# Four result buffers for the second layer, and a bias table loaded from two queues

## The reference, cut to what matters

```python
def _L0_conv_ref(x, qkv_w, qkv_b, proj_w, proj_b, rel_table):   # shifted-window attention
    bias = rel_table[idx].reshape(L, L, HEADS).transpose(2, 0, 1)      # L = 49, HEADS = 12
    xs = jnp.roll(x, shift=(-SHIFT, -SHIFT), axis=(1, 2))
    ...                                                     # windows of 7 x 7 tokens, 96 channels
    attn = jnp.einsum('bhqd,bhkd->bhqk', q * d ** -0.5, k) + bias[None] + mask
    out = jnp.einsum('bhqk,bhkd->bhqd', softmax(attn), v) @ proj_w.T + proj_b
    ...                                                     # rolled back
def _L1_conv_ref(x):
    s = box_sum(x, 2, 5)                                    # 5 places along the width
    num = box_sum(s * s, 3, 20)                             # 20 channels
    d = box_sum(box_sum(x * x, 2, 5), 3, 20)
    return jnp.nan_to_num(num / (d * norm), nan=1.0)

x = x + _L0_conv_ref(_gn(x), ...)          # x: (32, 56, 56, 96) float32, group norm per image
x = x + _L1_conv_ref(_gn(x))
```

## Time and profile before

| | |
|---|---|
| time, median of 3 runs | 3396.27 us (3393.39 to 3396.65) |
| the profiled execution: its time | 3382.73 us |
| its span, first to last instruction | 3380.9 us |
| PE busy | 3166.0 us, 94% of the span |
| DVE, ACT, POOL busy | 2784.9, 2375.2, 2263.3 us |
| mean granted TensorE clock | 0.982 |
| transfers in `q1` (all issued by SP) | 270.81 MB, 32.8% of 16 engines |

### The profile page before, as it was taken

One profiled execution on the slowest core, in us unless ns is written; L12 is line 12 of the kernel. 1 busy time (PEld: TensorE's weight loads), 2 busy tenths in 40 slices (PEclk: granted clock), 3 DMA queues, 4 the chain that ended last, 5 costly groups with the idle time before them and its releaser, 6 DMA issues.

```text
span 3380.9 us, 146870 instructions
## 1 busy us (share of the span) xinstructions
PE 3166.0 (94%) x60544; PEld 2620.4 (78%) x60544; DVE 2784.9 (82%) x4882; ACT 2375.2 (70%) x4705; POOL 2263.3 (67%) x2522
## 2 busy tenths in 40 slices
PE   3999999999999999999999999999999999999997
PEld 2778787887888778787778787778777777787785
DVE  4788888888888888888888888888888888888883
ACT  2567776777777777777777777777777777777764
POOL 3566666666677666677666667666667666677663
PEclk8999999999999999999999999999999999999995
DMA  3333333333333333333333333333333333332220
GB/s 74 82 89 80 87 92 77 85 89 84 87 91 84 84 93 80 84 93 81 84 93 80 87 92 81 83 93 81 85 92 81 84 92 81 86 92 71 73 63 23
DMA packets 385693, 280.20 MB, mean 83 GB/s; under 512 B 261927, under 2 KB 384904, under 8 KB 385032
## 3 DMA queue, kind: packets, MB, share of 16 engines
q1 hardware_dynamic: 385032, 270.81, 32.8%
HBM read 39.35 MB, written 38.54 MB: 23 GB/s over the span
## 4 chain that ended last, share of the span: by engine, by line
PE 47%; SPq 26%; DVE 8%; issue 6%; ACT 6%; DMA 5%; POOL 1%; DVEq 0%; ACTq 0%; POOLq 0%
SPq L317 10%; SPq L325 10%; PE pP L466 9%; PE pO L481 8%; PE pS L454 6%; DMA out<-tok_out 5%; SPq L330 5%; PE pM L555 3%; DVE T L816 3%; PE pM L549 3%; PE pM L566 3%; PE pM L504 3%; PE pM L394 2%; PE pM L388 2%; PE pM L436 2%
## 5 line engine op out<-in xcount | busy, mean ns | idle before, releaser
L1052 POOL TENSOR_TENSOR T<-T,MX 128x588 f32<-128x588 f32 x1024 | 1213.0, 1185 | 602.8 <-DVE MX L823 599.5
L816 DVE TENSOR_TENSOR T<-pS,table 128x588 f32<-128x588 f32 x1024 | 781.6, 763 | 353.8 <-PE pS L454 352.4
L663 ACT ACTIVATE P<-pP 128x588 f32<-128x588 f32 x1024 | 674.8, 659 | 258.7 <-PE pP L466 231.0
L466 PE MATMUL pP<-K,T 113*128 113x113 f32 x6144 | 789.4, 264 | 14.6 <-POOL T L1052 8.4
L823 DVE TENSOR_REDUCE MX<-T 128x12 f32<-128x588 f32 x1024 | 775.0, 757 | 17.9
L481 PE MATMUL pO<-V,P 128*49 128x18 f32 x24576 | 697.7, 198 | 46.1 <-ACT g L696 39.9
L481 PEld LDWEIGHTS pO<-V,P 128*49 128x49 f32 x24576 | 662.8, 126 | 53.0 <-ACT g L696 45.1
L466 PEld LDWEIGHTS pP<-K,T 113*128 113x128 f32 x6144 | 630.3, 143 | 71.0 <-issue 23.2
L1017 POOL TENSOR_TENSOR y<-Y 96x472 f32<-96x472 f32 x224 | 217.1, 969 | 491.6 <-ACT Y L740 491.6
L454 PE MATMUL pS<-KE,QS 128*64 128x196 bf16 (+1 forms) x8192 | 474.9, 233 | 19.8 <-DMA KE<-KS 13.5
L454 PEld LDWEIGHTS pS<-KE,QS 128*64 128x64 bf16 x8192 | 302.0, 109 | 135.4 <-issue 81.6
(11 more groups left out here) (94 smaller groups left out, 5904.0 us busy)
## 6 DMA issues: line engine op xcount, KB each, us to landing
KE<-KS SPq DMA_DIRECT2D x512, 147.0 KB
KS<-knh SPq DMA_DIRECT2D x768, 49.0 KB, 2.0
QS<-qnh SPq DMA_DIRECT2D x768, 49.0 KB
out<-tok_out SPq DMA_DIRECT2D x384, 84.0 KB
tok_in<-x SPq DMA_DIRECT2D x224, 84.0 KB
KS<-knl SPq DMA_DIRECT2D x384, 49.0 KB, 2.0
QS<-qnl SPq DMA_DIRECT2D x384, 49.0 KB
tok_in<-x SPq DMA_DIRECT2D x224, 63.0 KB
```

Source lines behind the costliest of these rows:

```text
L466: mm = pe.transpose(pP[:, c, QN * at:QN * at + QN], T[j % 4][0:QN, 2 * h:2 * h + 2, :], pick)
L663: act.activation(P32[j % 3][:, :, :].rearrange("p (c a w) q -> p c a (w q)", c=2, w=2), src, ACT.Exp).then_inc(p_made, 1)
L816: dve.tensor_tensor(T[j % 4][:, :, 0:L].rearrange("p (b h) k -> p b h k", b=2), pS[:, :, 0:HALF].rearrange("p b (h k) -> p b h k", k=L), t ...
L1052: pool.tensor_tensor(t, t, MX[j % 4][:, :].unsqueeze(2).broadcast_to([128, HEADS, L]), ALU.subtract).then_inc(shifted, 1)
```

## The change

There are four `tok_out` buffers and four `stored` semaphores instead of two; `result(G)` now waits for the stores of group G-4. SP issues four of the small transfers that start the semaphores instead of two. Of the 49 transfers of the bias table, the first 24 are issued by ACT, after its table load and ahead of everything else in its stream, and behind the same wait on `pool_fills`; SP issues the other 25 where it issued all.

```diff
+OUTS = 4
+BIAS_BY_ACT = 24
...
-        tok_out = [sb(f"tok_out{i}", [ROWS2, TILES, C]) for i in range(2)]
+        tok_out = [sb(f"tok_out{i}", [ROWS2, TILES, C]) for i in range(OUTS)]
...
-        stored = [signal(f"stored{i}") for i in range(2)]
+        stored = [signal(f"stored{i}") for i in range(OUTS)]
...
-            return 16 + 16 * sum(len(store_runs(k % GROUPS)) for k in range(G % 2, G, 2))
+            return 16 + 16 * sum(len(store_runs(k % GROUPS)) for k in range(G % OUTS, G, OUTS))
+
+        def load_bias(queue, q):
+
+            i, j = q // WIN, q % WIN
+            src = flipped[WIN - 1 - i:2 * WIN - 1 - i, WIN - 1 - j:2 * WIN - 1 - j, :]
+            queue.dma_start(bias_raw[q:q + 65:64, :, :].rearrange("p (i j) h -> p i (j h)", i=WIN),
+                            src.rearrange("(o i) j h -> o i (j h)", o=1).broadcast_to([2, WIN, WIN * HEADS])
+                            ).then_inc(bias_in, 16)
...
-                    sp.dma_start(dst, tok_out[G % 2][SIDE * h2:SIDE * h2 + SIDE, t:t + n, :]
-                                 ).then_inc(stored[G % 2], 16)
+                    sp.dma_start(dst, tok_out[G % OUTS][SIDE * h2:SIDE * h2 + SIDE, t:t + n, :]
+                                 ).then_inc(stored[G % OUTS], 16)
...
-            for i in range(2):
+            for i in range(OUTS):
 
                 sp.dma_start(tok_out[i][0:1, 0, :], pb_row).then_inc(stored[i], 16)
 
             sp.wait_ge(pool_fills, LOADS + 1)
-            for q in range(L):
-                i, j = q // WIN, q % WIN
-                ...
-                             ).then_inc(bias_in, 16)
+            for q in range(BIAS_BY_ACT, L):
+                load_bias(sp, q)
...
@@ scalar
+            act.wait_ge(pool_fills, LOADS + 1)
+            for q in range(BIAS_BY_ACT):
+                load_bias(act, q)
             act.wait_ge(ones_ended, 1)
             act.wait_ge(dve_setup, 3)
...
@@ vector, result(G)
-                dve.wait_ge(stored[G % 2], stores_before(G))
-                dve.tensor_tensor(tok_out[G % 2][:, :, :].rearrange("p t c -> p (t c)"),
+                dve.wait_ge(stored[G % OUTS], stores_before(G))
+                dve.tensor_tensor(tok_out[G % OUTS][:, :, :].rearrange("p t c -> p (t c)"),
                                   bankC[0:ROWS2, 0:TILES * C], numt[:, :], ALU.subtract).then_inc(out_made, 1)
```

More of the change, by code:

```diff
@@ L347, in _ @@
             sp.dma_start(PT[C:C + 1, :], pb_row).then_inc(consts_in, 16)
-            for i in range(2):
+            for i in range(OUTS):
                 sp.dma_start(tok_out[i][0:1, 0, :], pb_row).then_inc(stored[i], 16)
             sp.wait_ge(pool_fills, LOADS + 1)
-            for q in range(L):
-                i, j = q // WIN, q % WIN
-                src = flipped[WIN - 1 - i:2 * WIN - 1 - i, WIN - 1 - j:2 * WIN - 1 - j, :]
-                sp.dma_start(bias_raw[q:q + 65:64, :, :].rearrange("p (i j) h -> p i (j h)", i=WIN),
-                             src.rearrange("(o i) j h -> o i (j h)", o=1).broadcast_to([2, WIN, WIN * HEADS])
-                             ).then_inc(bias_in, 16)
+            for q in range(BIAS_BY_ACT, L):
+                load_bias(sp, q)
             sp.wait_ge(dve_fills, len(scores_operands))
@@ L370, in _ @@
                     store(G)
-            for i in range(2):
-                sp.wait_ge(stored[i], stores_before(ALL_GROUPS + (ALL_GROUPS - i) % 2))
+            for i in range(OUTS):
+                sp.wait_ge(stored[i], stores_before(ALL_GROUPS + (i - ALL_GROUPS) % OUTS))
         @block.tensor
```

## The result

| | before | after |
|---|---|---|
| time, median | 3394.83 us (3389.3 to 3396.65, 4 runs) | 3310.69 us (3308.44 to 3315.31, 4 runs) |
| ratio | | 0.9754, 95% interval 0.9739 to 0.977 |
| profiled execution, span | 3380.9 us | 3313.5 us |
| mean granted clock | 0.982 | 0.983 |

The change takes 84 us off the median, 67.4 off the profiled span. The forecast was 50, and the time lies 20 us under the low end of its range. In a later job the changed kernel took 3313.73 us against 3397.42, again 84 less (ratio 0.9751, 0.9732 to 0.9771).

A forecast was written before the change was run, and what follows sets the result against it. It took PE, busy 94%, and an about equally long loop through SP's queue as the bound. Buffers 40 us plus set-up 9.9 made 50 off the median 3396.27: 3346 us, range 3331 to 3370.

The forecast's parts named there:

- The loop through SP's queue: On SP, tok_out's store stands behind stage's 22 transfers, so result and PE's projection wait; one turn takes 25.9 us.
- the marks named for it: Profile signs: no result wait for stores, projection's wait under 5 us, PE idle near 165 us, SP's chain share under a tenth.
- the wait of `stage`: On SP, the idle time before stage, waiting for low_k, was to become shorter by some 40 us.
- steady part: In the loop of slots, four buffers remove PE's idle wait at the projection: 40 us, range 35 to 50.
- The rival on the clock: TensorE's lower clock after start-up lasts longer and makes the kernel slower, 3411 us; chance 0.05.
- The 0.2 us per wait: At the projection, DVE's 51.8 us less PE's 40.1, over 57 waits, read as DVE being ready ahead of PE.
- upper end: DVE's whole wait for tok_out stores ahead of result, 51.8 us, as the most the buffers could gain.
- The set-up: Before the loop, ACT's 24 bias transfers let turn_x(8) start earlier: 9.9 us gained, between 7.9 and 10.8.
- rival 1: In set-up, both queues share the path for issuing transfers, so nothing is gained there: 3356 us; chance 0.10.
- Rival 2: In the softmax ring, PE's next wait, for POOL's product, takes half of the 40 us: 3366 us; chance 0.15.
- The forecast's own low end: Fastest time with both parts at their upper ends: 3334 us, or 3331 with 3 us for the runs.
- the distances of 12.28 and 12.12 us: On DVE, spacings of successive results, the first without its wait; at most a tenth of a microsecond comes back.

The follow-up runs named there:

- the kernel with two buffers: The kernel before, its two buffers and set-up kept, with only SP's order within a slot changed so that store comes ahead of stage: 3321.57 us, ratio 0.9762.
- `bias_only`: The changed kernel put back to two output buffers, ACT still issuing 24 of the 49 bias transfers: 3390.36 us against 3399.21 before, ratio 0.9969.

## Why the prediction was wrong, point by point

**Where the stall was, and what it was made of: right.** The loop through SP's queue was found in the right rows, and the marks named for it came true: no wait of `result`, none of the projection, PE's idle time at 165 us, SP's share of the chain at 1%. The one mark that was missed is the wait of `stage`, shorter by 72.7 us instead of some 40. The order of SP's queue as the cause is shown by the kernel with two buffers.

**The size of the steady part: the step that failed.** The prediction said "PE is the engine that is nearly full and in order, so its own idle time is the price: I take 40". The buffers alone gave 74.7 us in the median, 59.8 in the profiles (61.2 without the 1.4 that its set-up lost). Of the 59.8, PE's idle time fell by 36.5 us, close to the 40, and its busy time, which the prediction held to be untouched ("work of PE, of which the change touches none"), by 23.3. What that term lacked are three things.

The first is the clock. A long halt of PE is often followed by a stretch at 1.2 GHz. In the profiled execution of before there were 23.9 us of it, worth up to 12 us, and these lie in PE's busy time, not in its idle time. The term counted idle time alone. The rival on the clock looked for this effect on the wrong side: it asked whether the change would bring such stretches, where the kernel before had them and the change took them away. The sentence "PE loses idle time by the change where the clock fell after idle time" was one step from it.

The second is that a halt costs more than its idle time shows. By the rows of before, from the start of the Q projection to that of the next scores (timeline of PE, line 394 to 454):

```profile
1507.61 0.34 PE L394 MATMUL pM<-XH,WH 97*96 97x392 bf16 x1
1507.79 0.33 PE L395 MATMUL pM<-XL,WH 97*96 97x392 bf16 x1
1507.95 0.33 PE L396 MATMUL pM<-XH,WL 97*96 97x392 bf16 x1
...
1508.71 0.46 PE L454 MATMUL pS<-KE,QS 128*64 128x196 bf16 x8
...
1520.93 0.34 PE L394 MATMUL pM<-XH,WH 97*96 97x392 bf16 x1
...
1521.77 0.37 PE L394 MATMUL pM<-XH,WH 97*96 97x392 bf16 x1 [0.17 <-DVE tok_out L916]
...
1522.40 0.46 PE L454 MATMUL pS<-KE,QS 128*64 128x196 bf16 x8
```

That is 1.10 us without a halt and 1.47 with one of 0.17: the halt costs 0.37, which is also what DVE waited there. A product's row is 0.33 us long, but the next starts 0.17 after it; the idle time begins only when the row has ended. Where two of these rows stand apart, their overlap is lost too, and the profile books it as busy time. The delays by hand say the same in the medians: 42.3 us for 32.2 of idle time and 74.7 for 62.8, which is 0.17 and 0.20 us more for each of 60 halts (in the profiles 42.4 and 64.7; the second shows hardly any). With 53 halts and 0.16 us each that is another 8 us. The 0.2 us per wait by which DVE's figure was above PE's, which the prediction put down to a DVE that was ready ahead of PE, is for the most part this overlap. So DVE's 51.8, given as the upper end, was nearer: 40 + 8 + 12 = 60, against the 61.2 of the profiles.

The third is the execution. Its 3382.73 us lie below every one of the 13 runs of before in the first job of the experiments, and its granted clock, 0.982, is as high as the highest of them; their median is 0.979. (On the chip of the last job before is faster, with a median of 3382.83.) The prediction saw that the median was 13.5 us above it and wrote that "none of the rows says that this difference would shrink". It was itself a part of the stall: 0.979 of 3399 us leaves 71 us of clock ungranted, 0.985 of 3324 leaves 50, so up to 21 us went by the clock in the timed runs, not 12. The other 54 are then the waits, 6 more than the 48 of the profile, as the profile of `bias_only` had more of them. One run of before, of 3377.87 us in the last job, had a clock of 0.985, as high as the kernels without store waits; it is still 53 us above the buffers alone, though on another chip. In the four jobs of the experiments the runs of before at a clock of 0.98 took 3387.01 to 3401.58 us, those at 0.977 3400.03 to 3412.99.

**The set-up: right, 1.1 us off at `turn_x(8)`.** It starts 8.8 us sooner instead of 9.9. ACT's issues took 13.89 / 24 = 0.579 us instead of the 0.541 taken. SP's first 18 took 9.70 us instead of 8.06, a fifth more, and its small ones 2.17 / 4 = 0.54 instead of 0.275; its 25 of the bias table, most of them issued when ACT was done, took 13.61 / 25 = 0.544 as before. So both are slower while both issue: SP was ready for the bias table 3.9 us later than before, 0.6 of it by the two more transfers, and its loads start at 31.42 instead of the 27.9 forecast. That is about a quarter of ACT's 13.9 us of issuing, where rival 1 wanted all of it. With the 2.37 us of the load's way to its first use the data are there at 33.8 by this estimate, just ahead of the 33.99 at which the norm lets PE go on; it was luck that this slip of 3.5 us didn't cost time as well. At the start PE could not begin until 16.95, and `keep_x(0)` came at 18.21 instead of 17.15. Part of the 8.8 was lost again in that execution, where the stretch at the lower clock that begins in the wait for `KE` was 34.1 us instead of 27.3 (in the second profile of the changed kernel it was 27.3 too); the first `result` is only 225.26 - 219.83 = 5.4 us sooner. The timed worth of this part is the 8.9 us of `bias_only`.

**The rivals.** Rival 2, the next wait in line, didn't come true for the buffers, where no wait of PE in the loop grew by more than 0.3 us (in the second profile of the changed kernel, one by 1.4), but did when the norm's wait was moved. The range took its lower end from DVE's wait as if that were all that could be won. It would have had to hold the difference between the runs and the profile as well. The forecast's own low end, given as 3334, comes out at 3332 by its terms (3396.27 - 50 - 10.8 - 3), and the distances of 12.28 and 12.12 us in the earlier trace rows are 0.16 apart, not "at most a tenth"; nothing hangs on either.

**Left open.** Why the clock fell at three of the five longest halts of before and not at the other two, and at 22 of 30 equal halts made by hand, isn't settled. The division of the 74.7 us of the median into 54 for waits and 21 for the clock is an estimate from the mean clocks; no profile of a slower run of before was taken.

## What to carry to other kernels

A queue that is served in program order makes a cheap transfer as late as everything issued ahead of it: moving one loop ahead of another on SP was worth as much here as the two added buffers. When you price a halt of TensorE, take the distance between the starts of the products on both sides, not the idle time, and see whether the granted clock falls at the halts; if it does, the products after them hold part of the price. If the profiled execution is faster than the timed runs, ask whether the stall that you are about to remove is what makes them differ.

## What the runs showed of the hardware

- After a halt of 1.31 to 2.20 us in an otherwise full TensorE there were 3.4 to 10.2 us at 1.2 GHz at 3 of 5 places in one execution, at 6 of 11 in another, and at 22 of 30 halts of 1.7 us made by hand. None followed the 60 halts of 1.05 us made by hand (62.8 us in all), nor the shorter ones in before and `bias_only`.
- Two engines that issue transfers at once slow each other: 0.579 us for one on ACT against 0.541 on SP alone, 18 loads on SP in 9.70 us instead of 8.06, and its smallest ones in 0.54 us instead of 0.275.
